# A macaron block (quantised FFN, 16-head attention, quantised FFN) on one core: first stage a period earlier in halves, projection chains spread, last stage and stores moved up

## What is computed

```python
def _L0_ffn_ref(x, weight, bias):            # x: rows of 128
    xq, xs = _mx_quantize(x2)                # blocks of 32, scale = max|block| / 7.5,
    wq, ws = _mx_quantize(w2)                # value = nearest point of an FP6 grid
    return (xq * xs) @ (wq * ws).T + bias
...
Q, K, V = x @ Wq + bq, x @ Wk + bk, x @ Wv + bv          # 16 heads of 8
scores = einsum("bhqd,bhkd->bhqk", Q, K) / sqrt(8)
scores = scores + 0.3 * log(mask + 1e-6)                 # mask: one 512 x 512 per head
attn = softmax(scores)
return (attn @ V) @ Wo + bo
...
x = x + 0.5 * _L0_ffn_ref(_layernorm(x), ...)
x = x + _L0_attn_ref(_layernorm(x), ...)
x = x + 0.5 * _L0_ffn_ref(_layernorm(x), ...)
```

## Time and profile before

| | us |
|---|---|
| median of 3 runs (lowest, highest) | 913.27 (909.49, 916.39) |
| profiled execution: its time | 915.71 |
| profiled execution: its span | 913.7 |
| PE busy (share of the span) | 729.2 (80%) |
| ACT busy | 672.3 (74%) |
| DVE busy | 532.2 (58%) |
| POOL busy | 187.4 (21%) |

### The profile page before, as it was taken

How to read it: one execution, slowest core, us unless ns; L and a number is a source line. 1 busy time by engine, 2 the same in 40 slices (tenths; PEclk the granted TensorE clock), 3 DMA queues, 4 the chain that set the end, 5 groups by cost and what they waited for, 6 DMA issues and landing times.

```text
span 913.7 us, 12885 instructions
## 1 busy us (share of the span) xinstructions
PE 729.2 (80%) x4355; PEld 257.3 (28%) x4355; DVE 532.2 (58%) x1308; ACT 672.3 (74%) x795; POOL 187.4 (21%) x164
## 2 busy tenths in 40 slices
PE   0367606899898888999879889999889888998944
PEld 0043300242222222433323224333233122322334
DVE  8776752764553376756784586567943323465264
ACT  1388734888787888888867888887768878888811
POOL 0306731103333110032252020133630000020011
PEclk9987755999999999999999999999999999999986
DMA  5639595643777674537776655477666655554201
GB/s 149 118 123 363 194 374 182 225 152 110 206 224 223 190 201 154 159 107 202 225 201 214 190 172 169 129 205 204 190 187 213 184 163 165 168 181 151 80 1 50
DMA packets 56068, 162.10 MB, mean 177 GB/s; under 512 B 14120, under 2 KB 24496, under 8 KB 45578
## 3 DMA queue, kind: packets, MB, share of 16 engines
q1 hardware_dynamic: 51740, 154.36, 55.1%
q0 software_dynamic: 1808, 5.94, 2.1%
q10 hardware_dynamic: 2446, 0.89, 0.6%
...
## 4 chain that ended last, share of the span: by engine, by line
PE 49%; DVE 15%; DMA 11%; ACT 11%; issue 9%; SPq 3%; POOL 1%; DVEq 0%; POOLq 0%; ACTq 0%
PE S_PS L1512 20%; PE O_PS L1526 17%; DVE S_PS L1148 8%; ACT BIG L682 7%; DMA BIG<-shift_rows 5%; PE F_PS L1417 3%; PE R_PS L1535 3%; DMA PART<-trig_parts 2%; ACT BIG L728 1%; DMA k_parts<-PART 1%; PE F_PS L1412 1%; SPq L331 1%; PE P_PS L1417 1%; SPq L334 1%; DMA q_parts<-PART 1%
## 5 line engine op out<-in xcount | busy, mean ns | idle before, releaser
L682 ACT ACTIVATE BIG<-S_PS 128x1024 f32<-128x1024 f32 x512 | 508.9, 1024 | 151.3 <-PE S_PS L1512 149.9
L1512 PE MATMUL S_PS<-BIG 98*128 98x512 bf16 x1024 | 303.9, 390 | 83.3 <-DVE S_PS L1148 47.0
L1526 PE MATMUL O_PS<-BIG,VX 128*9 128x512 f32 x2048 | 270.4, 601 | 0.9 <-issue 0.9
L1148 DVE COPY S_PS<-BIG 128x1024 f32<-128x1024 f32 x128 | 152.1, 1224 | 159.1 <-ACT BIG L682 157.5
L1512 PEld LDWEIGHTS S_PS<-BIG 98*128 98x128 bf16 x1024 | 74.6, 98 | 345.8 <-ACT BIG L682 128.8
L1161 DVE RECIPROCAL RD<-R_PS 128x16 f32<-128x16 f32 x64 | 16.4, 257 | 124.6 <-PE R_PS L1535 124.1
L533 POOL TENSOR_TENSOR XDT<-PART 128x512 bf16<-128x512 f32 x24 | 26.7, 1111 | 252.0 <-ACT PART L650 252.0
L1526 PEld LDWEIGHTS O_PS<-BIG,VX 128*9 128x9 f32 x2048 | 30.8, 88 | 112.2 <-issue 97.7
L510 POOL TENSOR_TENSOR BIG<-BIG,BFH 128x512 f32<-128x512 f32 x16 | 21.9, 1398 | 186.9 <-DVE BIG L980 134.5
L510 POOL TENSOR_TENSOR X<-X,BFH 128x512 f32<-128x512 f32 x16 | 26.0, 1652 | 151.0 <-DVE BIG L980 76.0
L542 POOL TENSOR_TENSOR PART<-PART 128x512 f32<-128x512 f32 x32 | 37.1, 1161 | 69.7 <-DVE PART L1051 68.5
...
## 6 DMA issues: line engine op xcount, KB each, us to landing
...
```

The source lines that it names most:

```text
L682: act.activation(E[:, m % 2, j, 2 * pair:2 * pair + 2, :], S_PS[:, pair, :, :], ACT.Exp, scale=LOG_WEIGHT)\
L1148: ve.tensor_copy(S_PS[:, pair, :, :], LNM[:, slot, 2 * pair:2 * pair + 2, :]).then_inc(s["seeded"], 1)
L1512: mm = pe.matmul(S_PS[:, pair, i, :], KT[0:ALL_ROWS, slot, K_COL[j], 128 * kb:128 * kb + 128], QT[0:ALL_ROWS, slot, j, :], start=False, st ...
L1526: mm = pe.matmul(O_PS[32 * j:32 * j + HD + 1, :], VX[:, slot_of(n), j, kb, h, :], E[:, m % 2, j, kb, :], start=kb == 0, stop=kb == T - 1)
```

## The change

`FIRST` stays for group 1 in period 0. For groups 2 and 3 the first stage moves one period ahead: `LATE[0]` does group 2 in period 0, `LATE[1]` group 3 in period 1, each in two halves of two batches (DVE's wide instructions become 128x1024, twice as many). All four batches use `F_PS` and `XDT[1]` one after the other; transpose, copy and product stand mostly at neighbouring ticks. Period 2 has no first stage. `CHAINS` keeps 48, 64, 80, 96 in period 0 and has 8, 40, 72, 96 in periods 1 and 2, with `norm` four ticks ahead of each chain. `LAST` starts at tick 24 instead of 50; its transpose, copy and product stand at neighbouring ticks; its FFN part is at ticks 73 to 91 instead of 104 to 127. SP's stores of the parts and of x follow, and POOL's list is written out anew.

```diff
@@ -78,15 +78,29 @@
              ffn_pe=(32, 34, 40, 42), add_ve=(33, 36, 41, 44), lnexp1_act=(39, 48), rstd1_ve=(40, 49),
              norm_ve=(42, 58, 74, 90))
 
-CHAIN = (48, 64, 80, 96)
-SECOND = dict(turn_pe=0, xnt_act=1, q_pe=4, q_act=5, k_pe=8, k_act=9, v_pe=12, v_ve=13, hi_q_ve=8, mid_q_ve=10,
-              hi_k_ve=11, mid_k_ve=13, norms_k_pe=14, k_top_ve=16, norms_q_pe=18, sq_ve=19, sqrt_act=21,
+
+LATE = ((dict(stats_ve=(52, 53), lnexp_act=55, rstd_ve=60, centre_ve=65, reduce_ve=66, scales_ve=68, to_grid_ve=73,
+              from_grid_ve=76, turn_pe=(80, 85), xd_copy_act=(81, 86), ffn_pe=(82, 87), add_ve=(84, 89),
+              lnexp1_act=91, rstd1_ve=92),
+         dict(stats_ve=(81, 82), lnexp_act=84, rstd_ve=94, centre_ve=97, reduce_ve=98, scales_ve=100, to_grid_ve=105,
+              from_grid_ve=108, turn_pe=(110, 115), xd_copy_act=(111, 116), ffn_pe=(112, 117), add_ve=(113, 118),
+              lnexp1_act=121, rstd1_ve=123)),
+        (dict(stats_ve=(42, 44), lnexp_act=46, rstd_ve=49, centre_ve=74, reduce_ve=75, scales_ve=80, to_grid_ve=81,
+              from_grid_ve=82, turn_pe=(93, 98), xd_copy_act=(94, 99), ffn_pe=(95, 100), add_ve=(97, 102),
+              lnexp1_act=104, rstd1_ve=107),
+         dict(stats_ve=(89, 90), lnexp_act=92, rstd_ve=96, centre_ve=99, reduce_ve=100, scales_ve=105, to_grid_ve=106,
+              from_grid_ve=108, turn_pe=(112, 117), xd_copy_act=(113, 118), ffn_pe=(114, 119), add_ve=(115, 120),
+              lnexp1_act=122, rstd1_ve=124)))
+
+CHAINS = ((48, 64, 80, 96), (8, 40, 72, 96), (8, 40, 72, 96), ())
+SECOND = dict(norm_ve=-4, turn_pe=0, xnt_act=1, q_pe=4, q_act=5, k_pe=8, k_act=9, v_pe=12, v_ve=13, hi_q_ve=8,
+              mid_q_ve=10, hi_k_ve=11, mid_k_ve=13, norms_k_pe=14, k_top_ve=16, norms_q_pe=18, sq_ve=19, sqrt_act=21,
               row_ve=24, turn_bound_pe=26, bound_act=27)
 
-LAST = dict(turn_pe=(50, 58, 66, 74), at_act=(51, 59, 67, 75), out_pe=(54, 62, 70, 78), add_ve=(57, 65, 73, 81),
-            centre_ve=83, lnexp_act=84, rstd_ve=88, reduce_ve=89, scales_ve=92, to_grid_ve=96, from_grid_ve=99,
-            turn_xd_pe=(104, 110, 116, 122), xd_copy_act=(105, 111, 117, 123), ffn_pe=(108, 114, 120, 126),
-            add_ffn_ve=(109, 115, 121, 127))
+LAST = dict(turn_pe=(24, 32, 40, 48), at_act=(25, 33, 41, 49), out_pe=(26, 34, 42, 50), add_ve=(27, 35, 43, 51),
+            centre_ve=52, lnexp_act=53, rstd_ve=56, reduce_ve=57, scales_ve=60, to_grid_ve=64, from_grid_ve=67,
+            turn_xd_pe=(73, 77, 81, 88), xd_copy_act=(74, 78, 82, 89), ffn_pe=(75, 79, 83, 90),
+            add_ffn_ve=(76, 80, 84, 91))
 
 
@@ -263,7 +277,8 @@
 
 
         def calls_of(n, k):
-            return 2 if k == 1 or (k == 2 and n == NQ - 1) else 1
+            halved = {0: range(2, NQ), 1: range(2 * NQ), 2: range(NQ - 1, NQ)}
+            return 2 if n in halved[k] else 1
...
@@ -275,8 +290,13 @@
         def epilogue_turned(n, j):
             return XDT[1 - j % 2] if is_short(n) and n == NQ - 1 else XDT[1]
 
+
+
         def first_bank(n, j):
-            return (P_PS, F_PS)[j % 2]
+            return F_PS if n in (2, 3) else (P_PS, F_PS)[j % 2]
+
+        def first_turned(n, j):
+            return XDT[1] if n in (2, 3) else XDT[j % 2]
 
         def chain_bank(n, j):
...
@@ -411,16 +431,14 @@
                 if m == 1:
                     lnm_stored(sp, 15)
                     load_x(2)
-                if q > 0 and i in (13, 14, 15):
-                    store(q - 1, i - 13)
-                if q > 1 and i == 0:
-                    store(q - 2, 3)
-                if q < NQ - 1:
-                    if i in (9, 11, 13, 15):
-                        store_shift(q + 1, (i - 9) // 2)
-                    if i in (7, 9, 11, 13):
-                        store_q(sp, q + 1, (i - 7) // 2)
-                        store_k(sp, q + 1, (i - 7) // 2)
+                if q > 0 and i in (11, 12, 13, 14):
+                    store(q - 1, i - 11)
+                for j, c in enumerate(CHAINS[q]):
+                    if i == (c + SECOND["bound_act"]) // STEPS:
+                        store_shift(q + 1, j)
+                    if i == (c + SECOND["norms_k_pe"]) // STEPS:
+                        store_q(sp, q + 1, j)
+                        store_k(sp, q + 1, j)
                 if more and i == NH - 1:
                     load_shift(sp, m + 1)
...
@@ -589,17 +606,30 @@
             load_shift(pool, 0)
             pool.wait_ge(s["val_ready"], 2 * HALF_TILES)
             pool.memset(VX[:, 1, :, :, :, HD:HD + 1], 1.0).then_inc(s["vx_ones"], 1)
-            for q in range(NQ):
-                after, before = q < NQ - 1, q > 0
-                if after:
-                    bias_before(q + 1)
-                    for j in range(QB):
-                        chain(q + 1, j)
-                        start_after(q + 1, j)
-                        if j == 2 and before:
-                            bias_after(q - 1)
-                elif before:
-                    bias_after(q - 1)
+            def batch(n, j):
+                chain(n, j)
+                start_after(n, j)
+
+            bias_before(1)
+            batch(1, 0)
+            batch(1, 1)
+            bias_before(2, range(0, 2))
+            batch(1, 2)
+            batch(1, 3)
+            bias_before(2, range(2, 4))
+            batch(2, 0)
+            batch(2, 1)
+            bias_after(0)
+            batch(2, 2)
+            bias_before(3, range(0, 2))
+            batch(2, 3)
+            bias_before(3, range(2, 4))
+            batch(3, 0)
+            batch(3, 1)
+            bias_after(1)
+            batch(3, 2)
+            batch(3, 3)
+            bias_after(2)
             bias_after(NQ - 1)
             general_path(pool, general)
...
@@ -624,15 +654,18 @@
 
             def xd_copy0(n, j):
                 act.wait_ge(s["xd_turned0"], n * QB + j + 1)
-                if j >= 2:
+                if n in (2, 3):
+
+                    act.wait_ge(s["ffn_psum0"], n * QB + j)
+                    if j == 0:
+                        act.wait_ge(s["ffn_psum1"], QB * (n - 2))
+                elif j >= 2:
                     act.wait_ge(s["ffn_psum0"], n * QB + j - 1)
                 elif j == 0 and is_short(n):
                     act.wait_ge(s["norms_q"], n * QB)
                 elif j == 1 and not is_short(n):
                     act.wait_ge(s["ffn_psum1"], n * QB)
-                elif j == 1 and n >= 3:
-                    act.wait_ge(s["ffn_psum1"], (n - 2) * QB)
-                copy(XDT[j % 2][:, :], first_bank(n, j)[:, :], "xd_copied0")
+                copy(first_turned(n, j)[:, :], first_bank(n, j)[:, :], "xd_copied0")
 
             def xnt_copy(n, j):
                 g = n * QB + j
...
@@ -973,7 +1011,7 @@
             def centre(n, f, e=0):
                 c, js, ts = quants(n, f, e, 0), batches_of(n, f, e), tiles_of(n, f, e)
                 if f == 0 and past(n):
-                    ve.wait_ge(s["xn_turned"], QB * n)
+                    ve.wait_ge(s["xn_turned"], QB * (n - 1) + js.stop)
                 if f == 1:
                     ve.wait_ge(s["at_turned"], QB * n + js.stop)
                 rows = "p j t n -> p (j t) n"
...
@@ -1419,20 +1481,22 @@
                 mm.then_inc(s[name], 1)
 
             def turn_xd0(n, j):
-                pe.wait_ge(s["quant0"], (n + 1) * K_QUANT)
-                if j >= 2:
+                pe.wait_ge(s["quant0"], (calls_before(n, 0) + j * calls_of(n, 0) // QB + 1) * K_QUANT)
+                if n in (2, 3):
+                    pe.wait_ge(s["ffn_added0"], n * QB + j)
+                    if j == 0:
+                        pe.wait_ge(s["ffn_added1"], QB * (n - 2))
+                elif j >= 2:
                     pe.wait_ge(s["ffn_added0"], n * QB + j - 1)
                 elif past(n):
                     pe.wait_ge(s["v_ready"], QB * n)
                     if not is_short(n):
                         pe.wait_ge(s["ffn_added1"], QB * n)
-                    elif j == 1 and n >= 3:
-                        pe.wait_ge(s["ffn_added1"], QB * (n - 2))
                 turn(first_bank(n, j), XC[:, j, :, :], "xd_turned0")
 
             def ffn0(n, j):
                 pe.wait_ge(s["xd_copied0"], n * QB + j + 1)
```

203 lines of the change are left out of this document (118 added, 85 removed).

## The result

The changed kernel takes 942.71 us (median of 4 runs, 937.82 to 944.78); the kernel before, beside it, 913.53 (909.49 to 916.39). The ratio is 1.033, with a 95% interval of 1.0288 to 1.0373. So it is slower, as forecast.

A forecast was written before the change was run, and what follows sets the result against it. No engine is full; the chain of waits bounds the kernel, PE having 49% of it. The terms 12 + 3.6 + 4.9 - 7 + 4.3 = +17.8, taken as +17, on the 913.3 us median gave 930 us; range 906 to 944.

The forecast's parts named there:

- Slower by over 1%, through positions, split seeds and new pairs: The forecast for the whole kernel: slower by over 1%, 930 us, own range 923 to 940; chance 0.60.
- worse: Part of the forecast, chance 0.1: loads 2 us late in eight light heads, DVE held up by POOL, 940 to 945.
- two signs of being wrong: Products at k=2 don't lengthen their heads, or periods 1 and 2 lose over 8 us each.
- The position table: PE piece's price by k: product 0.89 us, transpose 0.44 at k 1 to 5; last stage +12, first stage +3.6.
- Split seeds, +4.9: DVE's additions (2.2 us, twice) and small instructions (0.5 us, once) between two seeds delay the second seed: +4.9 us.
- The clock, chance 0.05 and +5: TensorE: one more clock fall in each period, +5 us, 935; 0.05 of the forecast's chance.
- POOL and DVE, counted as nothing: Grid halves of `LATE` held up by POOL's chain work, up to 8 us of DVE time, none of it counted.
- Late loads, kept at 3.5 a period: Stores of parts still hold up the loads for the head after the next; 3.5 us a period kept.
- Chains, -7: In periods 1 and 2 chains no longer overlap, except the last two: -3.6 us a period, -7 in two.
- new pairs, +4.3: Pieces of two stages sharing a k, less the old mutual hindrance: net +4.3 us, bounds zero and twice that.
- It evens out: Within 1%, 904 to 922: copy's wait, second seeds and new hindrances mostly hidden by load waits, 918 us; chance 0.25.
- spreading wins: Faster than 904.1 us: everything beyond table prices goes in periods 1 and 2, positions cheap, split seeds hidden, 901; chance 0.15.

## Why the prediction was right, and where it was short

*Slower by over 1%, through positions, split seeds and new pairs*: right in the direction and in the first two. The sum gave +17, it is +29. The forecast's own range, 923 to 940, is missed; 942.7 lies in the band of *worse* (940 to 945, chance 0.1), and the full range holds it by 1.3 us. *Worse* named late loads in eight light heads, which did not come, and DVE held up by POOL, which did, at another place. That the number is inside the range is in part luck. Of the two signs of being wrong, the first (products at k = 2 that cost nothing) did not show, and the second (periods 1 and 2 lose over 8 us each) did for period 1 (10.5) and not for period 2 (1.1).

*The position table*: right, and the best part of it. Period 3 was to have seeds 11.1 us apart, they are 11.20, seen in every kernel that has this table and gone in those that don't. The stage costs 10.4 us (4.97 and 5.46) instead of 9.4; the terms that were short are the copy's wait in the sets at 1, 2, 3 and the product's 1.0 for 0.89. Against it stood a clock fall in period 3 of before that the changed kernel doesn't have, and so the period grew by 2.9, not 4.9. That fall belongs to the profiled execution and is no merit of the change.

*Split seeds, +4.9*: the mechanism was right, and the hole too (2.2 forecast; 2.70 us at PE, 2.26 for the heads without a fall). The term was mis-sized for what follows a hole: 4.4 us in head 15 of period 0, 5.2 and 4.9 in the kernel before.

*The clock, chance 0.05 and +5*: the failed weighing. (At the 1.6 us of its own row, one more fall in each of four periods is 6.4.) In the profile PE's time at 1.2 GHz rose from 25 to 50 us. What such a stretch costs is read from a bare head with one, 11.57 instead of 9.96 with a mean clock of 0.85: 1.6 us for 0.3 x 11.5 = 3.5 us at half, 0.46 each. So 25 x 0.46 = 11 us by this estimate, about the distance between 930 and 942. It is an upper bound. Head 13 of period 1, with the same split seed, shows it: these are its rows in the changed kernel and in the one with bounds first and late stores:

```profile
500.71:515.34 14.63, 11.70 (x65) 3.52 (x65) 14.05 (x32) 9.76 (x13) 7.36 (x6) 0.88 0.20 68
```
```profile
494.23:508.88 14.65, 10.26 (x65) 3.47 (x65) 14.06 (x32) 9.67 (x13) 7.80 (x6) 1.00 0.40 131
```

The mean clock was 0.88 and 1.00, and the head is as long. DVE is busy for 14 us of it, which fits a head whose length DVE sets. With a clock of 0.79 (the run with the last stage of period 3 as before) it is 16.03. In heads 7 the falls stand inside the price given below: at mean clocks of 0.89 and 0.79 over 15.06 and 15.99 us, 10 us at half, up to 4.6 of their 8.0 us. So the parts of this account overlap and must not be added up. The forecast had cited the Trainium skill, "TensorE: Matmul & The Clock Gate": an idle stretch halves the clock. The changed kernel agrees (all eight falls at waits of 1.9 to 3.2 us); the kernel before has two falls that no long wait explains, and the head just shown has a wait of 2.7 us without a fall.

*POOL and DVE, counted as nothing*: the failed step. The delay was looked for in the wide grid halves of `LATE`, at 1.0 us for each of eight, and at `to_grid` of the last stage. Of the eight, two were held up, the `from_grid` halves at 247.6 and 302.3 us, by 0.83 us each (2.05 for 1.22). It struck the smallest instructions: 0.17 us became 1.2 us three times, as if each had to get past one of POOL's four additions (4.95 us together). The forecast had drawn on the Trainium skill, "SBUF — State Buffer", "Who interferes with whom": a DVE instruction with two SBUF inputs and a GpSimd one that reads SBUF exclude each other. The three instructions are of that kind, and the run with POOL's additions later agrees (0.17 us). They stood ahead of `reduce`, and both ahead of the bounds that PE waits for. Heads 7 cost 3.5 and 4.5 us more, the late load under the hole and the clock behind it included.

*Late loads, kept at 3.5 a period*: about right in what the profile shows, 4.5, 3.4 and 2.3 us where 3 to 5 were expected. But a further 4.2 us and more lay hidden under the wait for the bounds, and came up when that was taken away.

*Chains, -7, and new pairs, +4.3*: the first did not happen (387.2 us with spread chains, 385.7 with dense ones). Period 2 alone lost its first stage, which should have bought 2.65 us beside what the chains give; it is 1.1 us longer, heads 1 to 7 paying 10 us and heads 8 to 15 giving back 8.6.

*It evens out* and *spreading wins*: neither the copies' waits nor the new positions were hidden; the table was paid in full. The positions alone cost 4.9 us in period 3, seen from both sides. So both fall.

What stays open: the falls without a hole ahead of them, and how much of the 11 us is really on the path, since no run could switch the clock's falls off. The new pairs (+4.3, of which the forecast said that no row has them) were not taken apart: heads 5 and 9 of period 1 grew by 2.3 and 1.9 us, and no run gives each its cause.
